# Attention scores of a sequence in one slot in four PSUM banks, the denominator one slot earlier, products with the masked scores later

## The reference

```python
q = jnp.exp(split_heads(x @ Wq.T + bq)); k = jnp.exp(split_heads(x @ Wk.T + bk)); v = split_heads(x @ Wv.T + bv)
kv  = jnp.cumsum(k[:, :, :, None] * v[:, :, None, :], axis=1)
num = jnp.einsum('zsD,zsDd->zsd', q, kv)
den = jnp.sum(q * jnp.cumsum(k, axis=1), axis=-1, keepdims=True)
x = layernorm(x + merge_heads(num / den) @ Wo.T + bo)
outs = einsum(silu(x @ expert_gate) * (x @ expert_up), expert_down)      # all 32 experts
x = layernorm(x + sum(outs of the 8 chosen * topk_w) + shared_mlp(x))
```

## Time and profile before

| what | value |
|---|---|
| median of 3 runs | 503.45 us (502.72 to 505.17) |
| the profiled execution, its own time | 503.26 us |
| span of its instructions | 501.5 us |
| TensorE busy | 456.1 us, 91% of the span |
| VectorE, ScalarE, GpSimd busy | 70%, 56%, 55% |
| mean granted TensorE clock | 0.957 |

### The profile page before, as it was taken

One profiled execution on the slowest core, in us unless ns is written; L12 is line 12 of the kernel. 1 busy time (PEld: TensorE's weight loads), 2 busy tenths in 40 slices (PEclk: granted clock), 3 DMA queues, 4 the chain that ended last, 5 costly groups with the idle time before them and its releaser, 6 DMA issues.

```text
span 501.5 us, 10675 instructions
## 1 busy us (share of the span) xinstructions
PE 456.1 (91%) x3914; PEld 350.0 (70%) x3914; DVE 351.3 (70%) x907; ACT 280.0 (56%) x523; POOL 278.3 (55%) x208
## 2 busy tenths in 40 slices
PE   4868599999999999999999999999999999889991
PEld 2756487778767787778767777768767777667761
DVE  1436538696787869696787869696787868767643
ACT  3726224973478536873478526873478526644652
POOL 2581235754576445754576445754576445765691
PEclk9587579999999999999999999999999999999997
DMA  7300733335152624336152634336152624335610
GB/s 237 138 1 2 150 67 85 84 83 134 35 119 40 154 64 106 85 79 139 34 121 42 147 67 105 86 73 145 32 114 47 146 51 106 84 72 103 154 35 21
DMA packets 28596, 44.94 MB, mean 90 GB/s; under 512 B 1920, under 2 KB 10368, under 8 KB 28160
## 3 DMA queue, kind: packets, MB, share of 16 engines
q1 hardware_dynamic: 28544, 44.26, 38.4%
HBM read 41.64 MB, written 2.62 MB: 88 GB/s over the span
## 4 chain that ended last, share of the span: by engine, by line
PE 34%; DVE 30%; issue 12%; ACT 7%; POOL 6%; DMA 2%; DVEq 1%; ACTq 0%; SPq 0%; POOLq 0%
PE bank L289 32%; DVE units L765 6%; DVE hidden_lo L654 6%; POOL units L852 3%; ACT hidden_hi L517 3%; DVE stats L674 2%; DVE k_sum L808 2%; POOL rstd L876 2%; DVE x L686 2%; DVE probs L664 2%; DMA weight_wide<-weight_d 1%; ACT L536 1%; ACT units L536 1%; DVE out_sb L773 1%; POOL hidden_lo L890 1%
## 5 line engine op out<-in xcount | busy, mean ns | idle before, releaser
L852 POOL TENSOR_TENSOR units<-units,weight_wide 128x512 f32<-128x512 f32 x128 | 173.8, 1364 | 166.5 <-DVE units L765 153.1
L536 ACT ACTIVATE units<-bank 128x512 f32<-128x512 f32 x136 | 80.9, 595 | 86.7 <-PE bank L289 42.4
L654 DVE TENSOR_TENSOR hidden_lo<-units,hidden_hi 128x512 fp32r<-128x512 f32 x112 | 98.8, 882 | 34.4 <-ACT hidden_hi L517 34.2
L765 DVE TENSOR_TENSOR units<-bank,units 128x512 f32<-128x512 f32 x136 | 93.1, 684 | 41.6 <-ACT units L536 22.5
L517 ACT ACTIVATE hidden_hi<-units 128x512 fp32r<-128x512 f32 x136 | 85.7, 630 | 61.0 <-POOL units L852 50.5
L289 PE MATMUL bank<-hidden_hi,down_hi 128*128 128x512 f32 x136 | 58.3, 428 | 10.9 <-DVE hidden_lo L654 6.4
L289 PE MATMUL bank<-x_hi,gate_hi 128*128 128x512 f32 x136 | 63.9, 469 | 0.0
L289 PE MATMUL bank<-x_hi,up_hi 128*128 128x512 f32 x136 | 54.6, 401 | 1.5 <-ACT units L536 1.5
L289 PE MATMUL bank<-x_lo,gate_hi 128*128 128x512 f32 x136 | 54.5, 400 | 0.0
L289 PE MATMUL bank<-x_hi,gate_lo 128*128 128x512 f32 x136 | 54.3, 399 | 0.0
L289 PE MATMUL bank<-x_hi,up_lo 128*128 128x512 f32 x136 | 54.2, 398 | 0.0
(11 more groups left out here) (102 smaller groups left out, 707.2 us busy)
## 6 DMA issues: line engine op xcount, KB each, us to landing
weight_wide<-weight_d SPq DMA_DIRECT2D x64, 512.0 KB, 6.7
xT<-xT_in SPq DMA_DIRECT2D x8, 256.0 KB, 7.0
x_tok<-x_in SPq DMA_DIRECT2D x8, 256.0 KB, 7.0
out_dram<-out_sb SPq DMA_DIRECT2D x8, 256.0 KB, 2.3
weight_wide<-up_in SPq DMA_DIRECT2D x1, 1088.0 KB, 8.2
up_raw<-up_in SPq DMA_DIRECT2D x1, 1088.0 KB, 10.3
down_raw<-down_in SPq DMA_DIRECT2D x1, 1088.0 KB, 12.5
weight_d<-weightT SPq DMA_DIRECT2D x8, 64.0 KB, 1.6
```

The lines of the kernel that those rows point to most:

```text
L536: nc.scalar.activation(units[n % 3][:, :], up_banks[2 * n % 3][:, :], ACT.Silu).then_inc(silu_done, 1)
L654: V.tensor_tensor(hidden_lo[n % 3][:, :], units[n % 3][:, :], hidden_hi[n % 3][:, :].bitcast(F32), ALU.subtract).then_inc(hidden_lo_done, 1)
L765: V.tensor_tensor(units[n % 3][:, :], up_banks[(2 * n + 1) % 3][:, :], units[n % 3][:, :], ALU.mult).then_inc(gated_done, 1)
L852: G.tensor_tensor(units[n % 3][:, :], units[n % 3][:, :], weight_wide[:, (n - 1) % (2 * PIECE), :], ALU.mult).then_inc(hidden_done, 1)
```

## The change

From the second group on, the scores of a sequence go to four banks (`o_bank`, `work_bank`, `mid_banks`). Both pairs of sequence 0 are issued in slot 16, after a wait for `kv_copied` (the banks hold the chunk products until VectorE has copied them), and both pairs of sequence 1 in slot 1, after waits for the four products of sequence 0 and for the reciprocal (`inv_done`). `den` moves from slot 2 to slot 0 and writes `work_bank`; its reciprocal moves on VectorE from slot 3 to slot 0, and `inv_wide` on ScalarE from slot 3 to slot 2. `between_chunks` and `within_chunks` of sequence 0 stand in slot 2, those of sequence 1 in slot 3. GpSimd's product for the denominator moves from slot 16 to slot 15. Around the first expert blocks, the second group's `k_totals` and its GpSimd product move ahead of the routing of the first group, and `up` of slot 2 stands between the two halves of the scores.

```diff
         def score_bank(m, i):
-            return (mid_banks + up_banks + [y_bank] + mid_banks)[i] if m == 0 else mid_banks[i % 2]
-
-        def den_bank(m):
-            return work_bank if m == 0 else mid_banks[0]
+            return (mid_banks + up_banks + [y_bank] + mid_banks)[i] if m == 0 else ([o_bank, work_bank] + mid_banks)[i % QUADS]
...
             steps(0, 0, ffn=True)
             steps(-1, 14, front=True)
             steps(0, 1, ffn=True)
-            steps(-1, 14, mid=True)
+            steps(-1, 14, 16, mid=True)
             steps(-1, 15, 16, front=True)
-            steps(-1, 16, mid=True)
-            steps(0, 0, 1, mid=True)
-            steps(0, *range(2, SLOTS), ffn=True, mid=True, front=True)
+            steps(0, 0, mid=True)
+            steps(0, 2, ffn=True)
+            steps(0, 1, 2, mid=True)
+            steps(0, *range(3, SLOTS), ffn=True, mid=True, front=True)
...
-            def scores(m, pair):
-
-                b, q = divmod(2 * pair, QUADS)
-                if pair == 0:
-                    if m == 0:
-                        pe.wait_ge(bias_done, 1)
-                    pe.wait_ge(k_exp, reached(m + 1))
-                    pe.wait_ge(q_masked, reached(m + 1))
-                    pe.wait_ge(gate_exp, reached(m))
-                    pe.wait_ge(weightT_copied, reached(m))
-                elif m > 0:
-                    pe.wait_ge(probs_done, reached(SEQS * QUADS * m + 2 * pair))
-                elif pair == 3:
-                    pe.wait_ge(probs_done, 2)
+            def scores(m, b, quads):
+
                 for c in range(CHUNKS):
                     t = slice(b * SEQ + c * CHUNK, b * SEQ + (c + 1) * CHUNK)
                     for half in range(2):
-                        for i in range(2):
-                            rows = slice(32 * (q + i), 32 * (q + i) + 32)
-                            last = mm(score_bank(m, 2 * pair + i)[64 * half:64 * half + 64, 128 * c:128 * c + 128],
+                        for q in quads:
+                            rows = slice(32 * q, 32 * q + 32)
+                            last = mm(score_bank(m, QUADS * b + q)[64 * half:64 * half + 64, 128 * c:128 * c + 128],
...
+                    if m > 0:
+                        pe.wait_ge(probs_done, SEQS * QUADS * m + QUADS + 1)
...
+                    if mid:
+                        pe.wait_ge(probs_done, SEQS * QUADS * m + QUADS + 2)
...
-                if mid and n < 2:
-                    scores(m, 2 + n)
                 if mid and n == 0:
-                    between_chunks(m, 0)
-                if mid and n == 2:
-                    between_chunks(m, 1)
-                if mid and n == (1 if m == 0 else 2):
                     pe.wait_ge(qk_sum_done, reached(m + 1))
                     if m == 0:
                         pe.wait_ge(kv_copied, SEQS)
                     else:
-                        pe.wait_ge(probs_done, reached(SEQS * QUADS * m + 7))
+                        pe.wait_ge(probs_done, reached(SEQS * QUADS * m + 2))
                     for i in range(TILES):
-                        last = mm(den_bank(m)[:, HEADS * i:HEADS * i + HEADS],
+                        last = mm(work_bank[:, HEADS * i:HEADS * i + HEADS],
                                   k_sum[:, 128 * i:128 * i + 128], head_ones)
                     last.then_inc(den_ready, 1)
                 if mid and n == 1:
+                    if m == 0:
+                        pe.wait_ge(probs_done, 2)
+                        scores(m, 1, (2, 3))
+                    else:
+                        pe.wait_ge(probs_done, SEQS * QUADS * m + QUADS)
+                        pe.wait_ge(inv_done, m + 1)
+                        scores(m, 1, (0, 1))
+                        scores(m, 1, (2, 3))
+                if mid and n == 2:
+                    between_chunks(m, 0)
                     within_chunks(m, 0)
+                if mid and n == 3:
+                    between_chunks(m, 1)
...
-                if front and n >= 15:
-                    scores(f, n - 15)
+                if front and n == 16:
+                    if f == 0:
+                        pe.wait_ge(bias_done, 1)
+                    else:
+                        pe.wait_ge(kv_copied, SEQS * (f + 1))
+                        pe.wait_ge(weightT_copied, f)
+                    pe.wait_ge(k_exp, reached(f + 1))
+                    pe.wait_ge(q_masked, reached(f + 1))
+                    scores(f, 0, (0, 1))
+                    scores(f, 0, (2, 3))
+                    if f == 0:
+                        scores(f, 1, (0, 1))
...
-                if mid and n == 3:
+                if mid and n == 2:
...
-                if mid and n < 2:
-                    masked_probs(m, 2 + n)
+                if mid and n < 3:
+                    masked_probs(m, 1 + n)
+                if mid and n == 0:
+                    dve.wait_ge(den_ready, reached(m + 1))
+                    dve.wait_ge(inv_widened, reached(m))
+                    V.reciprocal(inv_den[:, :], work_bank[:, 0:TILES * HEADS]).then_inc(inv_done, 1)
...
-                if mid and n == 3:
-                    dve.wait_ge(den_ready, reached(m + 1))
-                    dve.wait_ge(inv_widened, reached(m))
-                    V.reciprocal(inv_den[:, :], den_bank(m)[:, 0:TILES * HEADS]).then_inc(inv_done, 1)
...
+                if front and f != 1 and n == 14:
+                    k_totals(f)
+                if m == 0 and mid and n == 8:
+                    k_totals(1)
...
-                if front and n >= 15:
-                    masked_probs(f, n - 15)
+                if front and n == 16:
+                    masked_probs(f, 0)
...
-                if front and n == (14 if f == 1 else 16):
...
+                if front and f != 1 and n == 15:
+                    q_times_totals(f)
+                if mid and m == 0 and n == 10:
+                    q_times_totals(1)
```

More of the change, by code:

```diff
@@ L758, in expert_weights, with k_totals @@
                                 ).then_inc(weight_done, 1)
+            def k_totals(f):
+                dve.wait_ge(k_exp, reached(f + 1))
+                dve.wait_ge(den_ready, reached(f))
+                for b in range(SEQS):
+                    k = kT[:, b * SEQ:(b + 1) * SEQ]
+                    V.tensor_tensor_scan(k_sum[:, b * SEQ:(b + 1) * SEQ], k, k, 0.0, ALU.add, ALU.bypass
+                                         ).then_inc(k_scanned, 1)
             def slot(n, g, u, ffn, mid, front, tail):
@@ L802, in slot @@
                     normalise(x1[1 - u], resid, mean_var, rstd1, x1_done)
-                if front and n == 14:
-                    dve.wait_ge(k_exp, reached(f + 1))
-                    dve.wait_ge(den_ready, reached(f))
-                    for b in range(SEQS):
-                        k = kT[:, b * SEQ:(b + 1) * SEQ]
-                        V.tensor_tensor_scan(k_sum[:, b * SEQ:(b + 1) * SEQ], k, k, 0.0, ALU.add, ALU.bypass
-                                             ).then_inc(k_scanned, 1)
+                if front and f != 1 and n == 14:
+                    k_totals(f)
+                if m == 0 and mid and n == 8:
+                    k_totals(1)
                 if front and n == 15:
@@ L843, in _, with q_times_totals @@
             G.memset(v_pair[:, :, :, :], 0.0).then_inc(zeroed, 1)
+            def q_times_totals(f):
+                pool.wait_ge(k_scanned, reached(SEQS * (f + 1)))
+                pool.wait_ge(q_exp, reached(f + 1))
+                G.tensor_tensor(k_sum[:, :], k_sum[:, :], qT[:, :], ALU.mult).then_inc(qk_sum_done, 1)
             def slot(n, g, u, ffn, mid, front, tail):
@@ L882, in slot @@
                                     ).then_inc(x1_lo_done, 1)
-                if front and n == (14 if f == 1 else 16):
-                    pool.wait_ge(k_scanned, reached(SEQS * (f + 1)))
-                    pool.wait_ge(q_exp, reached(f + 1))
-                    G.tensor_tensor(k_sum[:, :], k_sum[:, :], qT[:, :], ALU.mult).then_inc(qk_sum_done, 1)
+                if front and f != 1 and n == 15:
+                    q_times_totals(f)
+                if mid and m == 0 and n == 10:
+                    q_times_totals(1)
                 if ffn and n - 1 in POOL_LOWS:
```

## The result

The changed kernel takes 488.25 us (median of 4 runs, 487.99 to 488.89) against 503.46 (502.72 to 505.17): ratio 0.9695, 95% interval 0.9669 to 0.9721. Forecast were 493.0 us with a range from 488.5 to 499.5. The profiled execution took 488.35 us, its span is 486.5 us (before 501.5).

What follows compares the result with a forecast made beforehand. TensorE's matmuls and the gaps between them were taken to bound a group. Six steady groups at 1.5 us (9.0) plus 1.3 around the first expert blocks took 10.3 off 503.26: 493.0 us, range 488.5 to 499.5.

Steps and rivals of the forecast that it cites:

- (a): Slot 15's scores join those of slot 16: one packed block less, 0.11 us saved a group.
- (b): Before slot 16's scores: the old 0.48 us gap goes, a wait for `kv_copied` of 0.42 us replaces it.
- (c): `den` and its reciprocal in slot 0: ready before slot 1's scores with 0.5 us slack, costing nothing.
- (e): The turn in slot 4: `inv_wide` runs in slot 2, so the 0.45 us gap goes.
- (f): VectorE reaches `attnT` up to 1.77 us earlier; projection's 0.26 us gap goes, residual starts 1.5 us earlier.
- (g): `down` of slot 9: could come 1.75 us earlier, but a 0.25 us wait remains, so the lead is 1.5 us.
- The first expert blocks: Reordered list and earlier scans: attention work done at 72.6 in place of 73.94, a gain of 1.3 us.
- the bound I named for a gain of 0: First expert blocks: block 1's `hidden_lo`, waiting for a weighted product whose DMA lands at 61.40, holds the chain.
- given back: VectorE not 1.5 us earlier through slots 10 to 15, so the `kv_copied` wait grows: 498.4 us; chance 0.15.
- no effect: Steady groups trade one gap for another and the turn's gap returns as a later wait: 502.0 us; chance 0.06.
- the two slower ones: Queue: slot 1's scores wait for the late reciprocal, 508.0 us, chance 0.04; clock falls at paired scores, 514 us, 0.03.
- more: Clock rises early near 60 us and the `down` of slot 9 keeps no wait: 489.1 us; chance 0.17.

Runs made afterwards that it cites:

- the split in slot 1: Changed kernel, but in steady groups sequence 1's second pair of scores is issued behind the up matmuls of slot 2: 492.81 us, ratio 0.9780.
- alone: Kernel before with only den in slot 0 in the work bank, its reciprocal in slot 1, inv_wide in slot 2: 495.77 us, ratio 0.9833.
- the experiment: Changed kernel with the list around the first expert blocks as before, second group's scans and GpSimd product back at slot 14: 488.43 us.
- four quads: Changed kernel with all four quads of a sequence's scores taken in turn, not two and then two: 487.5 us, ratio 0.9662.

## Why the prediction was right in kind and 5 us short

(a), (b): the wait for `kv_copied` came as worked out, a gap of 0.52 us (216.60 to 217.12) for 0.42. A block less saves more than the 0.11 us at its end: a block that follows a big matmul without a wait also starts 0.33 us after it, not 0.24 (220.46 to 220.79 in the kernel before), so it is 0.2 us. The two errors cancel, and (a) and (b) gave about 0.15 us for 0.17.

(c) is the step that failed. "Two pairs of scores (2 x 1.03)" is the term: the block takes 1.54 us, twice a group, so 1.0 us a group was left out. Shown by the timeline, priced at 0.71 us with one block more by the split in slot 1. The trace of before held it: in the first group three pairs stood together and took 4.04 us to the next block at the low clock, where one pair's records last 1.98.

```profile
15.58 4.11 PE L289 MATMUL bank<-q_heads,kT 32*64 32x128 f32 x96
19.62 1.75 PE L289 MATMUL bank<-qT,kv_blocks 128*128 128x192 f32 x6
```

The same step said that the scores of slot 1 would not wait for the reciprocal, by 0.5 us. They did, for a gap of 0.43 us. TensorE asked 0.5 us earlier because of the shorter block. And step (c) started VectorE's part where `up` of slot 0 ends, without ScalarE's activation between them and what that waits for: `up` ended at 220.86, but `units` started at 221.78, behind the activation, which had waited for the second `hidden_lo`. Two `hidden_lo` took 1.05 and 1.23 us, not 0.69: each began while a weighted product ran on GpSimd (216.21 to 217.49, and 219.14 to 220.43) and ended some 0.55 us behind it. The second of these products stood behind the one for the denominator, which took 1.74 us. The rule of the Trainium skill weighed there ("SBUF — State Buffer", Who interferes with whom) agrees with these rows; I had priced them at nothing. Net of all, the scores gave 0.95 us a group for 0.17: 1.04 by the two shorter blocks, 0.34 lost again before slot 1's scores (a gap of 0.43 for the 0.09 of a block without a wait), 0.15 by (a) and (b), 0.09 by `den`, which starts without an entry gap where a pair had stood. These sum to 0.94.

(e), (f), (g): right as a mechanism, 1.55 us alone for 1.33. The rest is that a block which need not wait is also shorter: the turn by 0.06, the projection by 0.10 us. The wait of about 0.25 us before the `down` of slot 9 is there (0.3).

The first expert blocks: 1.3 us forecast; the start of slot 4 was right (72.77 for 72.6), its reasons were not. The list and the scans are worth nothing by the experiment. TensorE waited 2.22 us for the last products, behind a `hidden_lo` whose weighted product waited for its DMA, which was the bound I named for a gain of 0; the clock had risen near 61.8 and fell again near 65.2, at the end of that wait (granted clock 0.61 from 61 to 62 us, 1.00 from 62 to 65, 0.60 from 65 to 66), to rise for good near 68.6, where I had let it stay low to 69.5. These two and the shorter blocks happened to sum to my number.

Sum: six groups of 2.5 us are 15.0, the part up to the turn in slot 4 of group 0 gave 1.2 (76.14 to 74.97), and one wait of 1.03 us at 392.65, put down to "issue", took 1.0 back. That makes 15.2 of the span's 15.0; the groups at both ends of the six are not quite whole ones. The rivals "given back", "no effect" and the two slower ones did not come; "more" came by a cause that I had not listed.

## What to carry to other kernels

Time packed matmuls by the block, not by the instruction: look in the trace for a place where two or three such blocks already stand together and divide. Put work on other rows of the array side by side or in turn, with a bank for each quad; here four quads in turn take 1.14 us, two and two 1.54, and two apart 2.06. Each time TensorE gets faster, ask which result it will now ask for too early, and move that one up in its engine's list; a cost or a gain ahead of a wait is cut by the wait, so test a price behind it.

## What the runs showed of the hardware

Packed matmuls of 32 rows by 64 columns: a pair of quads alone 1.03 us; 0.87 more for the same pair again; 0.51 more for a pair on other rows and in other banks; eight tiles in turn 1.14 us for the work of both pairs. Why a third pair behind one on other rows adds 0.69 and not 0.51 us is open. Such a block in a stream of 128x512 matmuls costs 0.09 us at its start and 0.10 at its end besides.

A VectorE subtraction with both inputs in SBUF that began while GpSimd's product ran took 1.05 and 1.23 us, and 0.69 without one beside it; it ended some 0.55 us behind GpSimd's product each time.

Behind a wait, the turn and the projection took 0.06 and 0.10 us more than when they followed without one (0.66 and 1.16 us for 0.60 and 1.06).

At some places TensorE stood still for 1.0 us and more with no wait that the profile shows, each time within the matmuls with `probs`: once in the changed kernel, once with four quads (1.53 us), once and three times in the kernels with a repeated pair, not at all in the others:

```profile
392.65 0.76 PE L287 MATMUL bank<-probs,v_pair 128*32 128x64 f32 x38 [1.03 <-issue]
```

The cause is open. Whether these waits are what makes executions of one kernel differ by 1 to 3 us is not shown; each kernel has one profiled execution.
